# A vision transformer block on one core: patches and norm weights as half-precision parts, gates as value columns, stacked context parts, scores of four heads at once, a new order

## The chip, the cores and the metric

The program runs on one core of one Trainium2 chip. The time is the device time of that core for one launch, which computes 128 images; three runs of the kernel before are at hand. TensorE does the matrix products, VectorE, ScalarE and GpSimd (POOL in the rows) the rest, and SyncE issues the transfers.

## The reference

Each image of 224 x 224 x 3 is cut into 196 patches of 16 x 16, and the real part of each patch's Fourier transform, weighted, is projected to 192 numbers. With a class token that gives 197 tokens (T). Two layers follow, each added to what went in: attention with 12 heads of 16, whose softmax runs over the queries (`axis=2`), and attention with 12 heads of 64, with a norm on each head's queries and keys, and gates per head.

```python
x_fft = jnp.fft.rfft2(patches, norm='ortho').real            # times freq weights
out = jnp.concatenate([cls, x_flat @ proj_w.T + proj_b], axis=1) + pos_emb
# first layer, on _layernorm(h)
probs = jax.nn.softmax(scores, axis=2)                       # heads of 16
h = h + einsum('bhqk,bhke->bhqe', probs, v) @ Wo + bo
# second layer, on x = _layernorm(h)
q, k = _layernorm(q, w, b), _layernorm(k, w, b)              # per head of 64
attn = softmax((q * scale) @ k.T, axis=-1)
gates = softmax(x @ wg_w), top 2 of 10; softmax(x @ wg1_w); softmax(x @ wg0_w)
h = h + (gates * (attn @ v)) @ proj_w + proj_b
```

## The kernel before, in words

The tokens of an image lie in two chunks of 99 (TC); 198 (TP) columns hold both. Each of the five programs (`pe`, `dve`, `act`, `pool`, and SyncE's) runs a loop over the images, and the order of its steps is written out by hand in the table `ORDER`: `3:s1_0` is step `s1` number 0 of the image three ahead of the loop's own. So four images are in work at once, in different stages. Engines meet by semaphores alone: `made` waits until TensorE has filled a use of a PSUM bank, `read_out` and `room_for` until a reader has emptied it. The digits behind `@` in the table of `pe` are the banks (0 to 7) that a step fills. A step that waits holds up all that stands behind it on its engine.

The steps of an image, in the order of its data:

- `load` (SyncE) brings `xa` and `xb`, each pixel and its mirror, as 4 chunks of 98 rows (KC, KR). `fold` (VectorE, L877) adds them to `xs`, single precision. `tok` (TensorE) multiplies `xs` with `weff`, single precision, 4 chunks for each of the two token chunks. `tok` on VectorE (L883) adds positions and takes the moments for the layer norm (`moments`, L853 to L862): the statistics of two halves of a row, put together with six small instructions. `root1` (GpSimd, L440) is the inverse root. `nx1` (VectorE) normalises into two half-precision parts, high and low (`parts`).
- `x1T`, `qk1_0` to `qk1_2`, `v1`: transposes and products of the first layer. `mm5` forms a product of high and low parts in five half-precision passes (L491).
- `s1_0` to `s1_11`: scores of a head of the first layer, on 32 rows of the array, two heads at once, in four matmuls each. VectorE takes the maximum (L903), ScalarE the exponential with its sum (L733) into `p1`.
- `ctx_0` to `ctx_2`: VectorE scales `v1` by the inverse sums into `vs1` (L914, 16 of 32 columns per head, the rest zero), TensorE multiplies with `p1`, ScalarE copies the high part to `ctxT` and `cl` (L1015) the low part. `wo` (18 matmuls: high by high, low by high, high by low) and its moments (L924) follow, then `nx2`, `x2T`.
- `qk0` to `qk5`, `sq` (GpSimd, L479) and `ms` (mean squares of the heads), `var0` to `var2` (L759 to L764 on ScalarE, L984 to L988 on VectorE: an inverse root with one refinement step), then `rstd` (TensorE spreads the roots by `sel_rstd`) and `qkn` (L996, VectorE: times the weight `ln_w`, times `qkc`), `bias` (GpSimd, L484).
- `gl` (10 matmuls with 14 columns) gives the gate logits; `gl` and `gate` on VectorE make the gates from them.
- `v2` (values), `s2`, maximum (L1002) and exponential (L771) of the second layer, `gr` (gate over sum), `sc` (GpSimd, L475), `pT` (transposes, L672), `o2`, `ol`, and `proj`, which ends in the result and the store.

Outside the loop the weights are loaded and split once. The program is filled and drained by rounds of the same loop in which steps of images that don't exist are left out (`run_phases`).

## Time and profile before

| | us |
|---|---|
| median of three runs | 5535.41 (5534.62 to 5535.42) |
| span of the profiled execution | 5532.4 |
| TensorE busy in it | 5344.4 |
| VectorE busy | 4923.8 |
| ScalarE busy | 4327.1 |
| GpSimd busy | 2985.7 |
| one image in the loop (`tok` to `tok`) | 42.01 |

All times are of one execution on the one core. A busy time is the time in which at least one instruction of the engine is in work, so instructions that overlap count once; the mean length of an instruction is therefore longer than the distance from one to the next. In a timeline, instructions of one kind that follow each other stand in one row with their count, and the distance of two rows' starts is what the first of them took of the engine.

### The profile page before, as it was taken

How to read it: one execution, taken by the hardware profiler on the slowest of the kernel's cores; microseconds unless marked ns; L12 is line 12 of the kernel's file. 1: busy time of each engine (PE TensorE's matmuls, PEld its weight loads, DVE VectorE, ACT ScalarE, POOL GpSimd, SP SyncE). 2: the span in 40 equal slices, each digit the busy share in tenths (PEclk: the TensorE clock that was granted, in tenths of full speed). 3: DMA queues.
4: the chain of work that ended last, by engine and by line, in shares of the span. 5: the costliest groups of instructions: out<-in, count | busy, mean ns of one | idle time of the engine just before them, and what ended most of it. 6: DMA issues, size and time to landing. Idle time of an engine off the chain costs nothing.

```text
span 5532.4 us, 202492 instructions
## 1 busy us (share of the span) xinstructions
PE 5344.4 (97%) x63024; PEld 4563.7 (82%) x63024; DVE 4923.8 (89%) x16193; ACT 4327.1 (78%) x17409; POOL 2985.7 (54%) x3206
## 2 busy tenths in 40 slices
...
GB/s 72 18 22 18 17 21 17 18 17 21 18 17 21 17 18 17 21 18 17 21 18 17 20 18 18 17 21 18 17 21 17 18 17 21 18 17 21 18 17 6
...
## 3 DMA queue, kind: packets, MB, share of 16 engines
...
q14 instruction: 26, 0.21, 0.0%
...
## 4 chain that ended last, share of the span: by engine, by line
PE 94%; DVE 4%; issue 1%; ACT 0%; POOL 0%; SPq 0%; DVEq 0%; DMA 0%; POOLq 0%; ACTq 0%
PE bank L491 82%; PE bank L672 10%; PE bank L529 2%; DVE qk L898 1%; DVE qkn L996 1%; SPq L403 0%; ACT p L733 0%; DMA bp<-in_bp 0%; ACT pq L771 0%; POOL pq L475 0%; DVEq L902 0%; DVEq L1025 0%; DVE wqk_mean L804 0%; DVEq L992 0%; DVE nmax L903 0%
## 5 line engine op out<-in xcount | busy, mean ns | idle before, releaser
L475 POOL TENSOR_TENSOR pq<-pq,gn 99x788 f32<-99x788 f32 x768 | 1153.3, 1502 | 914.0 <-DVE gn L1011 913.9
L771 ACT ACTIVATE pq<-bank,nmax 99x197 f32<-99x197 f32 x3072 | 1300.1, 453 | 291.6 <-DVE nmax L1002 291.6
L733 ACT ACTIVATE p<-bank,nmax 99x197 f32<-99x197 f32 x3072 | 1323.1, 467 | 112.0 <-DVE nmax L903 97.3
L484 POOL TENSOR_TENSOR qkb<-qkn,ln_b 128x396 f32<-128x396 f32 x768 | 639.5, 847 | 1164.0 <-DVE qkn L996 1151.4
L777 ACT ACTIVATE pT<-bank 99x394 f32<-99x394 f32 x1536 | 767.6, 518 | 259.4 <-PE bank L672 256.4
L903 DVE TENSOR_REDUCE nmax<-bank 99x2 f32<-99x394 f32 x1536 | 843.2, 563 | 113.9 <-PE bank L491 101.7
L1002 DVE TENSOR_REDUCE nmax<-bank 99x2 f32<-99x394 f32 x1536 | 827.2, 559 | 25.7 <-PE bank L491 10.7
L733 ACT ACTIVATION_READ_ACCUMULATOR p<-bank,nmax 99x1 f32 x3072 | 762.6, 248 | 0.0
L491 PE MATMUL bank<-x2T,wqkc 128*128 128x198 f16 (+1 forms) x7680 | 752.5, 248 | 1.0 <-ACT p L733 0.7
L672 PE MATMUL bank<-ident,pq 99*99 99x99 f32 (+1 forms) x6144 | 725.3, 253 | 7.7 <-ACT pq L771 5.2
L771 ACT ACTIVATION_READ_ACCUMULATOR pq<-bank,nmax 99x1 f32 x3072 | 720.7, 235 | 0.0
L479 POOL TENSOR_TENSOR sq<-qkc 128x396 f32<-128x396 f32 x768 | 645.5, 848 | 103.0 <-ACT qkc L745 96.5
L491 PEld LDWEIGHTS bank<-x2T,wqkc 128*128 128x128 f16 (+1 forms) x7680 | 654.8, 97 | 51.5 <-issue 33.1
L672 PEld LDWEIGHTS bank<-ident,pq 99*99 99x99 f32 (+1 forms) x6144 | 626.7, 166 | 64.3 <-issue 38.3
L491 PE MATMUL bank<-qkb 64*99 64x197 f32 x6144 | 672.2, 345 | 6.8 <-POOL qkb L484 6.8
L996 DVE SCALAR_TENSOR_TENSOR qkn<-bank,ln_w,qkc 128x198 f32<-128x198 f32 x1536 | 568.2, 417 | 44.3 <-PE bank L491 38.0
L491 PE MATMUL bank<-pT,v 128*64 128x197 f32 x6144 | 600.8, 337 | 0.0
L491 PEld LDWEIGHTS bank<-qkb 64*99 64x99 f32 x6144 | 462.1, 162 | 135.9 <-issue 78.6
L491 PEld LDWEIGHTS bank<-pT,v 128*64 128x64 f32 x6144 | 407.7, 137 | 141.4 <-issue 72.9
L491 PE MATMUL bank<-wv,x2T 128*99 128x384 f16 (+1 forms) x2560 | 491.6, 331 | 0.0
L491 PE MATMUL bank<-qk 32*99 32x197 f16 x6144 | 374.4, 254 | 75.9 <-DVE qk L898 69.0
L782 ACT ACTIVATE oT<-bank 128x197 f16<-128x197 f32 x768 | 277.3, 361 | 169.1 <-PE bank L491 169.1
...
## 6 DMA issues: line engine op xcount, KB each, us to landing
xa<-in_xa SPq DMA_DIRECT2D x128, 300.1 KB
xb<-in_xb SPq DMA_DIRECT2D x128, 300.1 KB
out_tokens<-res SPq DMA_DIRECT2D x128, 74.2 KB
out_tokens<-res SPq DMA_DIRECT2D x128, 73.5 KB
...
```

The source lines that it names most:

```text
L475: nc.gpsimd.tensor_tensor(pair, pair, factor, op=ALU.mult).then_inc(s_sc.up(), 1)
L479: nc.gpsimd.tensor_tensor(sq[:, t], qkc[:, t], qkc[:, t], op=ALU.mult).then_inc(s_sq.up(), 1)
L484: nc.gpsimd.tensor_tensor(qkb[:, t], qkn[:, t % QKN_SLOTS], ln_b[:].unsqueeze(2).to_broadcast([128, 2, TP]), op=ALU.add).then_inc(s_qk.up( ...
L491: return nc.tensor.matmul(o, l, r, start=first, stop=last)
L672: last = nc.tensor.transpose(o[0:TC, k * T + c * TC:k * T + c * TC + n], pq[0:n, h % SLOTS, c, k * TC:k * TC + TC], ident[0:n, 0:n])
L733: last = nc.scalar.activation(p1[0:TC, h, c, :], psum("s1", h)[0:TC, c * T:c * T + T], ACT.Exp, bias=nmax1[:, c, h:h + 1], accum_out=sum1[ ...
L771: last = nc.scalar.activation(pq[0:TC, h % SLOTS, c, 0:T], psum("s2", h)[0:TC, c * T:c * T + T], ACT.Exp, bias=nmax2[:, h, c:c + 1], accum ...
L777: nc.scalar.activation(pT[0:TC, h].rearrange("p a b -> p (a b)"), psum("pT", h)[0:TC, 0:2 * T], ACT.Copy).then_inc(free("pT", h), 1)
L782: nc.scalar.activation(oT[:, t, 0, 0:T], psum("o2", t)[:, 0:T], ACT.Copy).then_inc(s_oh.up(), 1)
L903: V.tensor_reduce(nmax1[:, :, h], psum("s1", h)[0:TC, 0:2 * T].rearrange("p (a b) -> p a b", a=2), op=ALU.max, axis=AX.X, negate=True).the ...
L996: last = V.scalar_tensor_tensor(qkn[:, t % QKN_SLOTS, s, :], psum("rstd", t)[:, s * TP:s * TP + TP], ln_w[:, s:s + 1], qkc[:, t, s, :], AL ...
L1002: V.tensor_reduce(nmax2[:, h, :], psum("s2", h)[0:TC, 0:2 * T].rearrange("p (a b) -> p a b", a=2), op=ALU.max, axis=AX.X, negate=True).the ...
```

## The change

It has seven parts.

- **Patches.** The folded rows are laid out as 4 chunks of 128 rows instead of 98: three full ones, and the remaining rows twice in the fourth. `fold` moves to GpSimd and adds in place; a new step `xhi` (ScalarE) writes the half-precision high part `xh`, a new step `xlo` (GpSimd) the low part `xl`. `weff` is split the same way (`weff`, `weff_low`, scaled by 256). `tok` on TensorE becomes 22 half-precision matmuls instead of 8 single-precision ones (16 in the trace, which shows each as two).
- **Norm weights.** `ln_w` is multiplied into `sel_rstd` as two half-precision parts at the start, so that `qkn` is one product of 396 columns instead of two of 198 with a weight.
- **Gates.** The 14 columns of the gate weights stand behind the second layer's value weights: `gl` on TensorE goes, two of the four `v2` get 398 columns, and VectorE reads the logits from `v2`.
- **Context.** `vs1` holds each head's 16 columns twice, so that one product gives them on 32 rows; `cl` subtracts the high part from the lower half alone, `ctxT` then holds both parts in one operand, and `wo` has 12 matmuls.
- **First scores.** `s1` takes four heads at once, in four banks.
- **Moments.** The halves' statistics are put together by the aggregate instruction.
- **Order.** The table is new; `tok` runs four images ahead, and SyncE's loop is in the table too.

```diff
 def tok(img, _):
-    pe.wait_ge(*s_fold.at(img, 1))
+    pe.wait_ge(*s_xl.at(img, 1))
     for c in range(2):
-        for k in range(KC):
-            last = mm(o[0:TC, c * D:c * D + D], xs[:, k, c * TC:c * TC + TC], weff[:, k, :], k == 0, k == KC - 1)
+        tokens = slice(c * TC, c * TC + TC)
+        products = [(xh[:, 3, tokens], weff[:, 3, :]), (xl[:, 3, tokens], weff[:, 3, :])]
+        for k in range(KC - 1):
+            products += [(xh[:, k, tokens], weff[:, k, :]), (xh[:, k, tokens], weff_low[:, k, :]), (xl[:, k, tokens], weff[:, k, :])]
...
+def fold(img, _):
+    pool.wait_ge(*s_load.at(img, 32))
+    nc.gpsimd.tensor_tensor(xa[:], xa[:], xb[:], op=ALU.add).then_inc(s_fold.up(), 1)
+def xlo(img, _):
+    pool.wait_ge(*s_xh.at(img, 1))
+    nc.gpsimd.tensor_tensor(xl[:, :, 1:T], xa[:], xh[:, :, 1:T], op=ALU.subtract).then_inc(s_xl.up(), 1)
...
+def xhi(img, _):
+    act.wait_ge(*s_fold.at(img, 1))
+    if not isinstance(img, int) or img > 0:
+        act.wait_ge(*made(img - 1, "tok", 0))
+    nc.scalar.activation(xh[:, :, 1:T], xa[:], ACT.Copy).then_inc(s_xh.up(), 1)
...
 def s1(img, h):
-    if h % 2:
+    if h % GROUP:
         return
-    heads = (h, h + 1)
+    heads = range(h, h + GROUP)
...
 def wo(img, _):
-        for n, (x, w) in enumerate(((0, 0), (1, 0), (0, 1))):
+        for w in range(2):
             for g in range(3):
-                last = mm(o[0:TC, c * D:c * D + D], ctxT[:, g, x, c * TC:c * TC + TC], wo1[:, w, g, :], n + g == 0, n + g == 4)
+                last = mm(o[0:TC, c * D:c * D + D], ctxT[:, g, 1, c * TC:c * TC + TC], wo1[:, w, g, :], w + g == 0, w + g == 3)
...
 def v2_(img, n):
-    last = mm5(o[0:TC, 0:384], lambda k, r: wv2[r, k, 384 * a:384 * a + 384], lambda k, r: x2T[r, k, c, :], False)
+    cols = 384 + a * NG
+    last = mm5(o[0:TC, 0:cols], lambda k, r: wv2[r, k, 384 * a:384 * a + cols], lambda k, r: x2T[r, k, c, :], False)
...
 def moments(img, layer, src, name):
-    V.tensor_tensor(both[n][:], halves[:, :, 0, 1:3], halves[:, :, 1, 1:3], op=ALU.add)
...
+    V.memset(vare[n][:], LN_EPS)
+    for c in range(2):
+        last = V.bn_aggr(both[n][:, c, :], stats[n][:, c, :])
+    step(last, img, name, 2)
+    V.tensor_tensor(vare[n][:], both[n][:, :, 1], vare[n][:], op=ALU.add).then_inc(s_mv[layer].up(), 1)
...
 def rstd_(img, t):
-    for s in range(2):
-        last = V.scalar_tensor_tensor(qkn[:, t % QKN_SLOTS, s, :], psum("rstd", t)[:, s * TP:s * TP + TP], ln_w[:, s:s + 1],
-                                      qkc[:, t, s, :], ALU.mult, ALU.mult)
+    V.tensor_tensor(qkn[:, t % QKN_SLOTS].rearrange("p a b -> p (a b)"), psum("rstd", t)[:, 0:2 * TP],
+                    qkc[:, t].rearrange("p a b -> p (a b)"), op=ALU.mult).then_inc(free("rstd", t), 1)
...
 def load(img, _):
-    sp.wait_ge(*s_fold.at(img, 0))
+    sp.wait_ge(*s_xl.at(img, 0))
...
 ORDER, "pe":
-3:s1_6@15 1:s2_6@06 2:qk2@4 1:rstd5@7 1:pT_2@2 2:qk3@1 2:gl@0 3:s1_8@34 2:qk4@7 2:qk5@0 1:pT_3@6 3:s1_10@53 1:s2_8@12
+2:qk2@3 2:qk3@6 1:pT_6@4 3:s1_4@1572 1:pT_7@3 2:qk4@0 2:qk5@6 1:s2_10@31 1:o2_0@4 1:o2_1@5 1:o2_2@7 2:ms0@6 2:ms1
```

Three places of the order follow. A built program shows single-precision matmuls once, where the trace shows two; `s1` writes from `qk` (tile `qk1`), `s2` from `qkb`, the transposes `pT` from `ident,pq`, `qk` from `x2T,wqkc`.

TensorE before, the scores of two pairs of heads (`s1_8`, `s1_10`) in the middle of the loop:

```order
L491 MATMUL bank<-x2T,wqkc 128x198 x10
L491 MATMUL bank<-wgate,x2T 99x14 x10
L491 MATMUL bank<-qk 99x197 x8
L491 MATMUL bank<-x2T,wqkc 128x198 x20
L672 MATMUL bank<-ident,pq 99x99
L672 MATMUL bank<-ident,pq 99x98
L672 MATMUL bank<-ident,pq 99x99
L672 MATMUL bank<-ident,pq 99x98
L491 MATMUL bank<-qk 99x197 x8
L491 MATMUL bank<-qkb 99x197 x4
```

TensorE after, the scores of `s1_4` to `s1_7`:

```order
L521 MATMUL bank<-x2T,wqkc 128x198 x20
L698 MATMUL bank<-ident,pq 99x99
L698 MATMUL bank<-ident,pq 99x98
L698 MATMUL bank<-ident,pq 99x99
L698 MATMUL bank<-ident,pq 99x98
L521 MATMUL bank<-qk 99x197 x16
L698 MATMUL bank<-ident,pq 99x99
L698 MATMUL bank<-ident,pq 99x98
L698 MATMUL bank<-ident,pq 99x99
L698 MATMUL bank<-ident,pq 99x98
L521 MATMUL bank<-x2T,wqkc 128x198 x20
L521 MATMUL bank<-qkb 99x197 x4
```

Two groups of eight matmuls with other work between them became one group of sixteen; the gate product `wgate` is gone.

GpSimd before, the squares and the products with the gates (`sc`), then the roots of the layer norms and the first `bias` steps of the next round:

```order
L479 TENSOR_TENSOR sq<-qkc 128x396 x3
L475 TENSOR_TENSOR pq<-pq,gn 99x4x197
L479 TENSOR_TENSOR sq<-qkc 128x396
L475 TENSOR_TENSOR pq<-pq,gn 99x4x197 x2
L440 TENSOR_TENSOR rstd<-vare,mhalf 99x2
L484 TENSOR_TENSOR qkb<-qkn,ln_b 128x396 x2
L440 TENSOR_TENSOR rstd<-vare,mhalf 99x2
L484 TENSOR_TENSOR qkb<-qkn,ln_b 128x396
L452 TENSOR_TENSOR h1b<-h,bo 99x192 x2
```

GpSimd after, the end of a round of its list, from `sc4` to `sc1` of the next:

```order
L505 TENSOR_TENSOR pq<-pq,gn 99x4x197 x2
L514 TENSOR_TENSOR qkb<-qkn,ln_b 128x396
L458 TENSOR_TENSOR xa<-xa,xb 128x784
L514 TENSOR_TENSOR qkb<-qkn,ln_b 128x396
L490 TENSOR_TENSOR h2b<-h,bp 99x192 x2
L514 TENSOR_TENSOR qkb<-qkn,ln_b 128x396
L463 TENSOR_TENSOR xl<-xa,xh 128x4x196
L514 TENSOR_TENSOR qkb<-qkn,ln_b 128x396 x2
L505 TENSOR_TENSOR pq<-pq,gn 99x4x197 x2
```

The fold and the low part stand between the `bias` steps (`qkb`), and all of these come behind one another.

VectorE before, around the refinement of the head variance (`lnvar` to `rs_hl`, step `var2`), with the low parts of the contexts ahead and `rsum`, `gn` (step `gr5`) behind:

```order
L1015 TENSOR_TENSOR ctxT<-bank,ctxT 128x197 x3
L1019 TENSOR_TENSOR oT<-bank,oT 128x197
L1002 TENSOR_REDUCE nmax<-bank 99x2
L877 TENSOR_TENSOR xs<-xa,xb 98x4x196
L984 SCALAR_TENSOR_TENSOR lnvar<-bank,rootsq 128x198
L986 SCALAR_TENSOR_TENSOR rootsq<-lnvar,root 128x198
L987 TENSOR_SCALAR rs_mask<-rootsq,low_rows 128x198
L988 SCALAR_TENSOR_TENSOR rs_hl<-rootsq,rs_mask 128x198
L1008 RECIPROCAL rsum<-sum 99x4
L1011 TENSOR_TENSOR gn<-rsum,mg 99x4
L1019 TENSOR_TENSOR oT<-bank,oT 128x197
L924 SCALAR_TENSOR_TENSOR h<-bank,h1b 99x384
```

VectorE after, the same step:

```order
L1056 TENSOR_TENSOR oT<-bank,oT 128x197
L1044 RECIPROCAL rsum<-sum 99x4
L1047 TENSOR_TENSOR gn<-rsum,mg 99x4
L1056 TENSOR_TENSOR oT<-bank,oT 128x197 x2
L1022 SCALAR_TENSOR_TENSOR lnvar<-bank,rootsq 128x198
L1024 SCALAR_TENSOR_TENSOR rootsq<-lnvar,root 128x198
L1025 TENSOR_SCALAR rs_mask<-rootsq,low_rows 128x198
L1026 SCALAR_TENSOR_TENSOR rs_hl<-rootsq,rs_mask 128x198
L1056 TENSOR_TENSOR oT<-bank,oT 128x197
L1015 TENSOR_SCALAR v<-bank 99x384
L1033 TENSOR_TENSOR qkn<-bank,qkc 128x396
L929 COPY x1T<-bank 128x396
```

The fold ahead of it is gone; behind it stand now the low part of an output, a `v2` and the first `qkn` of the same image, for which TensorE needs the result of this step.

## Rows read from the trace of the kernel before

**Rows 1.** The page, part 1: busy time, share of the span and instructions of each engine.

```profile
PE 5344.4 (97%) x63024; PEld 4563.7 (82%) x63024; DVE 4923.8 (89%) x16193; ACT 4327.1 (78%) x17409; POOL 2985.7 (54%) x3206
```

**Rows 2.** One steady image: stretch, length, busy by engine, clock, DMA share, GB/s.

```profile
2422.77:2464.78 42.01, 41.45 (x495) 35.47 (x493) 38.08 (x127) 33.77 (x138) 23.26 (x25) 1.00 0.06 18
```

**Rows 3.** Timeline of TensorE: start, length (us), line, operation, tiles, [idle before].

```profile
2410.23 0.60 PE L491 MATMUL bank<-wgate,x2T 128*99 128x14 f16 x10
2410.76 0.54 PE L491 MATMUL bank<-qk 32*99 32x197 f16 x8
2411.23 1.91 PE L491 MATMUL bank<-x2T,wqkc 128*128 128x198 f16 x20
...
2418.90 0.85 PE L491 MATMUL bank<-p,vs 128*32 128x197 f32 x16
2419.68 0.89 PE L491 MATMUL bank<-pT,v 128*64 128x197 f32 x8
2420.51 0.94 PE L672 MATMUL bank<-ident,pq 99*99 99x99 f32 x8
2421.28 1.65 PE L491 MATMUL bank<-wo,ctxT 128*99 128x192 f16 x18
2422.77 2.77 PE L491 MATMUL bank<-weff,xs 98*99 98x192 f32 x16
2425.38 0.51 PE L672 MATMUL bank<-ident,pq 99*99 99x99 f32 x4
2425.72 0.33 PE L491 MATMUL bank<-rs_hl,sel_rstd 128*128 128x198 f16 x2
...
2432.24 1.02 PE L491 MATMUL bank<-wv,x2T 128*99 128x384 f16 x5
2433.10 0.52 PE L529 MATMUL bank<-ident,parts 99*128 99x99 f16 x8
2433.45 3.14 PE L491 MATMUL bank<-wp,oT 128*99 128x192 f16 x36
...
2439.05 0.76 PE L491 MATMUL bank<-qk 32*99 32x197 f16 x16 [0.56 <-DVE qk L898]
2439.74 0.91 PE L491 MATMUL bank<-qkb 64*99 64x197 f32 x8
```

**Rows 4.** Timeline of VectorE, same columns, from the fold to a layer norm.

```profile
2421.22 0.97 DVE L877 TENSOR_TENSOR xs<-xa,xb 98x784 f32<-98x784 f32 x1
2422.10 0.36 DVE L984 SCALAR_TENSOR_TENSOR lnvar<-bank,rootsq 128x198 f32<-128x198 f32 x1
...
2423.71 0.18 DVE L1008 RECIPROCAL rsum<-sum 99x4 f32<-99x4 f32 x1
...
2425.55 0.16 DVE L857 TENSOR_TENSOR both<-stats 99x4 f32<-99x4 f32 x1
...
2426.36 1.45 DVE L996 SCALAR_TENSOR_TENSOR qkn<-bank,ln_w,qkc 128x198 f32<-128x198 f32 x4
2427.73 0.55 DVE L883 TENSOR_TENSOR h<-bank,posb 99x384 f32<-99x384 f32 x1
```

**Rows 5.** Timeline of VectorE, one pair of the `vs` products.

```profile
2412.26 0.83 DVE L914 TENSOR_TENSOR vs<-v,rsum 99x64 f32<-99x64 f32 x2
```

**Rows 6.** Timeline of GpSimd at the same time.

```profile
2412.02 0.85 POOL L479 TENSOR_TENSOR sq<-qkc 128x396 f32<-128x396 f32 x1
```

**Rows 7.** Groups by line and shape, VectorE: busy us, mean ns of one, idle before.

```profile
L914 DVE TENSOR_TENSOR vs<-v,rsum 99x64 f32<-99x64 f32 x384 | 154.5, 402 | 23.8
...
L914 DVE TENSOR_TENSOR vs<-v,rsum 98x64 f32<-98x64 f32 x384 | 82.0, 214 | 0.0
```

**Rows 8.** The page, part 5: GpSimd's longest product, same columns.

```profile
L475 POOL TENSOR_TENSOR pq<-pq,gn 99x788 f32<-99x788 f32 x768 | 1153.3, 1502 | 914.0 <-DVE gn L1011 913.9
```

**Rows 9.** Timeline of ScalarE, the head variance and what follows.

```profile
2420.05 0.42 ACT L759 ACTIVATE lnvar<-bank,eps 128x198 f32<-128x198 f32 x1
...
2421.18 0.48 ACT L777 ACTIVATE pT<-bank 99x394 f32<-99x394 f32 x1
```

More of the change, by code:

```diff
@@ L60, in fold_pairs, with fold_rows @@
     return np.array(first), np.array(mirror)
+def fold_rows(rows):
+    out = np.zeros((KC * KR, *rows.shape[1:]), np.float32)
+    out[:3 * KR] = rows[:3 * KR]
+    rest = rows[3 * KR:]
+    for part in range(2):
+        out[3 * KR + 64 * part:3 * KR + 64 * part + len(rest)] = rest
+    return out
 def fold_basis():
@@ L137 @@
+3:v1@4 1:pT_1@2 1:pT_2@3 1:s2_6@56 1:pT_3@0 2:x2T@2 3:qk1_2@3 1:s2_8@10 2:qk0@2 2:qk1@5 1:pT_4@4 1:rstd5@6 1:pT_5@2
+2:qk2@3 2:qk3@6 1:pT_6@4 3:s1_4@1572 1:pT_7@3 2:qk4@0 2:qk5@6 1:s2_10@31 1:o2_0@4 1:o2_1@5 1:o2_2@7 2:ms0@6 2:ms1
+2:ms2 3:ctx0@0 1:o2_3@4 4:x1T@3 2:v2_0@1 1:pT_8@5 2:rstd0@7 1:pT_9@2 1:pT_10@6 1:pT_11@4 2:rstd1@5 3:s1_8@2137
+1:o2_4@0 1:o2_5@6 2:s2_0@54 2:v2_1@0 2:v2_2@2 2:rstd2@6 2:v2_3@1 2:rstd3@0
 """,
     "dve": """
-3:fold 1:var2 0:gr5 0:ol1 2:wo 1:rstd0 1:rstd1 3:tok 0:ol2 0:ol3 0:ol4 3:nx1 0:ol5 1:s2_0 1:s2_1 1:gate3 1:s2_2 1:s2_3
@@ L149 @@
 """,
     "pool": """
-3:root1 1:bias2 3:h1b 1:h2c 2:h2b 1:sc0 1:sc1 1:bias3 2:sq0 1:sc2 2:sq1 1:bias4 1:bias5 2:sq2 2:sq3 2:sq4 1:sc3 2:sq5
-1:sc4 1:sc5 3:root2 2:bias0 2:bias1
+0:sc0 0:sc1 1:root2 0:h2c 2:h1b 0:sc2 0:sc3 1:sq0 1:sq1 1:sq2 0:bias5 3:root1 1:sq3 1:sq4 1:sq5 0:sc4 0:sc5 1:bias0
+4:fold 1:bias1 1:h2b 1:bias2 4:xlo 1:bias3 1:bias4
+""",
+    "sp": """
+4:load 0:store
 """,
```

184 lines of the change are left out of this document (92 added, 92 removed).

## The prediction

> **What bounds the kernel now.** I read the busy shares first, then one steady image, then the waits inside it. The page puts TensorE at 97% of the span, VectorE at 89%, ScalarE at 78%, GpSimd at 54% [rows 1]. The ends matter little with 128 images, so the number to explain is the length of one image in the loop, from one `tok` to the next: 42.01 us [rows 2]. In it TensorE is busy 41.45 us, VectorE 38.08, ScalarE 33.77, GpSimd 23.26, and the granted clock is 1.00, the 2.4 GHz level [rows 2]. What TensorE does not do in that time is 0.56 us, and the timeline shows it as one wait, ahead of the sixteen `s1` matmuls, for VectorE's `qk1` [rows 3]. So work taken off TensorE shortens the image, until VectorE (91% full) or a hand-over between engines takes its place. The span is 5532.4 us against a median of 5535.4, so 3 us are added at the end; 128 images of 42.01 are 5377.3, which leaves 155.1 us for loading, preparing, filling and draining.
>
> **TensorE, part by part.** Costs are taken from the start of one group to the start of the next, because a matmul's own length overlaps its neighbours.
> `tok`: 2422.77 to 2425.38, 2.61 us in single precision [rows 3]. After, it is 22 half-precision products with 192 moving columns. The 18 of `wo` have that shape and run from 2421.28 to 2422.77, 1.49 us or 0.083 each [rows 3]. 22 x 0.083 = 1.82: minus 0.79.
> `wo`: 18 become 12: minus 0.50.
> `gl`: 2410.23 to 2410.76, 0.53 us, disappears [rows 3]. Ten `v2` matmuls get 14 more columns, at 0.083/192 us a column 0.06: minus 0.47.
> `s1`: a pair of heads alone takes 2410.76 to 2411.23, 0.47 us, and stands alone four times in the image; the two pairs that follow each other take 2439.05 to 2439.74, 0.69 us [rows 3]. That is 4 x 0.47 + 0.69 = 2.57. After, there are three groups of four heads. What a group costs no row shows exactly. It can't be under the 0.47 of a pair, since each head still has four matmuls behind each other; the nearest upper row is the 0.69 of two pairs one after the other. So the term lies between 1.41 and 2.07. I take 0.47, because in the 0.69 row the second pair's instructions stand behind all of the first pair's, while the new loop alternates the four heads, as the pair alternates its two: minus 1.16, at worst minus 0.50.
> `ctx` keeps its 32 columns per head, so its matmuls cost what they did; folding the norm weights into `sel_rstd` changes no matmul. I count 21 changes of tile shape (full, row parts, column parts) in the order of before and 20 after, and take them as equal.
> Sum: 41.45 - 0.79 - 0.50 - 0.47 - 1.16 = 38.5 us of TensorE work an image; 39.2 with the dear `s1`.
>
> **The other engines.** VectorE loses the fold, 2421.22 to 2422.10: minus 0.88 [rows 4]. Its twelve `qkn` products (four in 2426.36 to 2427.73, 0.34 each) become six of 396 columns; the 384-column `h` shows 0.55 as a length, so six take at most 3.3 instead of 4.1, and less where they follow closely [rows 4]: minus 0.8 to 1.2, I take 1.0. The two layer norms run from `both` to the next work in 2425.55 to 2426.36, 0.81 us, with six small instructions [rows 4]; after it is four. The aggregate of the statistics stands in no row: as cheap as the small ones the saving is 0.54 for both layers, with a longer one it is nothing; I take 0.5. The scaled `vs` doubles its 64 columns in six instructions; from 0.21 for 64 [rows 7] to 0.55 for 384 a column costs 1.06 ns, so plus 0.4. VectorE: 38.08 - 0.88 - 1.0 - 0.5 + 0.4 = 36.1 us, 92% of a 39.2 us image: nearly as full as now. Gates read from SBUF and the other edits of `tok` and `cl` keep their shapes: zero.
> ScalarE gets `xhi`, 784 columns, some 1.0 us as twice the 0.48 of a 394-column copy [rows 9]: 34.8. GpSimd gets the fold and `xlo`, each near the 1502 ns of its 788-column product [rows 8]: 26.3 of 39.2, 67%. Behind `fold` and `xlo` on GpSimd stand `bias1` to `bias4`, for which `s2` waits; at 12 us of slack an image I put no cost on them. SP's loads now wait for `xlo` and stand in one queue with the stores; `fold` comes at the end of the next round of GpSimd's list, most of an image after the store that the load stands behind, so nothing. They carry 128 rows for 98.
>
> **What is late next.** The order is new, so every cushion is. The narrowest that I find is the head variance. TensorE's `ms2` ends, ScalarE does `var0` and `var1` (2420.05 to 2421.18, and 0.1 to finish: 1.2 us [rows 9]), VectorE does `var2` (2422.10 to 2423.71, 1.5 to 1.6 [rows 4]), and TensorE's `rstd0` waits for that: 2.8 us, and three hand-overs. Before, `ms2` ends at 2418.90 and `rstd0` starts at 2425.72, 6.8 us later [rows 3]. After, five steps stand between them: `ctx` 0.78, `o2` 0.83, `x1T` 0.35, `v2` 0.86, `pT` 0.34 [rows 3], 3.16 in all. That leaves 0.0 to 0.4, if VectorE is free at once. Besides, four banks must be free at each `s1` group where two were enough. The waits of TensorE lie between nothing and some 2 us an image (every `s1` group and `rstd0` late by 0.5). I take 0.7, near the 0.56 that the row of before shows, because the engine that makes TensorE wait is as full as it was.
>
> **The time.** 38.5 + 0.7 = 39.2 us an image, 128 of them 5018. Filling and draining: 155 now; one more phase, and fold, `xhi` and `xlo` ahead of the first `tok` (4 us) against shorter phases: 130 to 170, I take 150. With the 3 us of the median: 5018 + 150 + 3 = 5171, say **5170 us**, 6.6% less.
>
> **Rivals.**
> *No wait is left.* TensorE goes through in 38.5: 128 x 38.5 + 153 = 5081. For it: one wait in an image now. Against: the 3.16 us cushion.
> *Four heads don't run at once.* Then `s1` costs 0.69 or more a group, the image 39.9, the time 5260. For it: the only row with two pairs together. Against: the alternation.
> *VectorE stands behind GpSimd and becomes the bound.* At 2412.26 VectorE's pair of `vs` products, with two SBUF inputs, takes 0.83 us, and GpSimd is in `sq` from 2412.02 for 0.85, so until 2412.87 [rows 5, 6]. Over the run the first of such a pair takes 402 ns, the second 214 [rows 7]: 0.19 more, three times an image. After, GpSimd is busy for 67% instead of 55%, with longer instructions, and such products (three `vs`, two `parts`, two in `var2`) meet it in other places. If seven are held by 0.6 us, less the 0.56 paid now, VectorE needs 36.1 + 3.6 = 39.7, and with 0.6 of its own waits the image is 40.3, the time 5311. The Trainium skill, SBUF — State Buffer, section "Who interferes with whom", says that a VectorE instruction with two SBUF inputs and a GpSimd instruction that reads SBUF shut each other out, the second waiting for the whole of the first; this trace agrees (0.83 us ending with `sq`). By that rule the new placing alone decides, which the rows can't tell.
> *Slower: the four banks.* If TensorE stands at each `s1` group until the fourth bank has been read, and nothing behind it may pass, then 42.05 - 38.5 = 3.5 us of waiting, 1.2 at each of three groups, makes the time equal to now (5535), and 1.5 at each gives an image of 43.0 and 5657. For it: the single wait of the trace is at such a group [rows 3]. Against: it is 0.56, and the banks are taken by work that ends a microsecond and more ahead. The Trainium skill, TensorEngine Tiling (Array Packing), "Gotcha 1: PSUM Pressure", warns of this: different row tiles write different banks. Here a row shows 0.56 for two pairs and none shows four taken at once.
>
> **Chances.** Forecast (image 38.9 to 39.6, 5130 to 5220) 0.47; no wait 0.25; `s1` dear 0.08; VectorE behind GpSimd 0.13; the four banks 0.04; about the same time, by several small delays, 0.03. Differences under 0.2% can't be told from none. Faster 0.93, same 0.03, slower 0.04. The range runs from 5060 (38.4 us, filling 145) to 5315, which takes in all rivals but the slower ones and the outer halves of two.
>
> **What would show it.** In the profile after: the image from `tok` to `tok` at 39.2; `tok` near 1.8 us, `wo` 1.0, a group of sixteen `s1` matmuls near 0.5 (0.69: the dear case); VectorE near 36 us busy an image; TensorE's waits at `rstd` behind VectorE's `rs_hl` or at `s1`, 0.7 us together. VectorE at 97% or more, `vs` with a mean above 0.6, would be the lock; waits above 1 us at each `s1` group the banks. I am wrong if the image stays above 40 with TensorE idle, or if the granted clock falls below the upper level in the loop.

## The result: slower, 6117.6 us, and the profile after

The changed kernel takes 6117.57 us (median of 4 runs, 6116.84 to 6117.92) beside 5535.1 for the kernel before on the same chip: 1.1052 times as long, interval 1.1037 to 1.1068. Forecast was 5170, and 5060 to 5315 as range. An image takes 46.64 us instead of 42.01.

The page of after, part 1, answers [rows 1]; then one steady image from one `tok` to the next, in the columns of [rows 2]:

```profile
PE 5135.4 (84%) x61744; PEld 4202.8 (69%) x61744; DVE 5640.8 (92%) x14799; ACT 4465.3 (73%) x17537; POOL 3433.0 (56%) x3462
```

```profile
3019.06:3065.70 46.64, 39.79 (x485) 32.57 (x484) 43.80 (x116) 34.86 (x138) 26.75 (x28) 1.00 0.06 20
```

TensorE's work did shrink (41.45 to 39.79 us busy), ScalarE and GpSimd have what was forecast (34.86, 26.75), and the clock stays at 1.00, the 2.4 GHz level. VectorE, forecast at 36.1 us, is busy for 43.80. TensorE is idle for 6.85 us an image, no longer in one wait as in [rows 3] but in waits of six kinds. Its waits over the whole run (us in total, times, longest):

```profile
PE bank L521 <- ACT p L766: 273.7, 248, 2.3
PE bank L521 <- DVE oT L1056: 199.2, 250, 1.4
PE bank L521 <- DVE qkn L1033: 118.7, 126, 2.4
PE bank L521 <- DVE ctxT L1051: 118.3, 126, 1.8
PE bank L563 <- DVE parts L913: 105.4, 129, 6.0
PE bank L521 <- DVE rs_hl L1026: 54.3, 128, 0.9
```

Five of them name VectorE. The first names ScalarE's `p`, which itself stood 951.1 us behind VectorE's `nmax` (page, part 5):

```profile
L766 ACT ACTIVATE p<-bank,nmax 99x197 f32<-99x197 f32 x3072 | 1276.9, 433 | 951.2 <-DVE nmax L939 951.1
```

So the waits lead to VectorE. VectorE itself is idle for 2.84 us of the image, 1.67 of it in one wait for ScalarE's `pq`. It has not more instructions than before (14799 for 16193) but longer ones. Its groups by line and shape, the columns of [rows 7]:

```profile
L1047 DVE TENSOR_TENSOR gn<-rsum,mg 99x4 f32<-99x4 f32 x768 | 499.9, 651 | 26.3
L909 DVE TENSOR_SCALAR x<-h,both,rstd 99x192 f32<-99x192 f32 x512 | 396.6, 814 | 1.5 <-POOL rstd L468 1.5
L951 DVE TENSOR_TENSOR vs<-v,rsum 98x128 f32<-98x128 f32 x384 | 315.7, 822 | 0.0
L912 DVE CAST parts<-x 99x384 f16<-99x384 f32 x256 | 275.5, 1076 | 8.8
L1024 DVE SCALAR_TENSOR_TENSOR rootsq<-lnvar,root 128x198 f32<-128x198 f32 x128 | 120.5, 941 | 4.4
L983 DVE TENSOR_TENSOR glog<-v,gmax 99x20 f32<-99x20 f32 x128 | 103.8, 811 | 0.0
```

In the trace of before, `gn` of the same shape took 166 ns, `x` 374, the conversion 386, `rootsq` 367. Instructions that read PSUM did not grow (`nmax` 559 ns, as before; `qkn`, whose shape is new, 560). Nor did GpSimd's own products (`pq` 1504 ns for 1502, `sq` 851 for 848): the standing still is VectorE's. One `gn`, a product of four columns, on VectorE's timeline, and GpSimd's at the same time (start, length, as [rows 3]):

```profile
3040.14 0.18 DVE L1044 RECIPROCAL rsum<-sum 99x4 f32<-99x4 f32 x1 [1.67 <-ACT pq L804]
3040.36 1.81 DVE L1047 TENSOR_TENSOR gn<-rsum,mg 99x4 f32<-99x4 f32 x1
3042.09 1.98 DVE L939 TENSOR_REDUCE nmax<-bank 99x2 f32<-99x394 f32 x4
```

```profile
3038.89 2.46 POOL L509 TENSOR_TENSOR sq<-qkc 128x396 f32<-128x396 f32 x3
3041.30 0.85 POOL L514 TENSOR_TENSOR qkb<-qkn,ln_b 128x396 f32<-128x396 f32 x1
3042.11 0.70 POOL L468 TENSOR_TENSOR rstd<-vare,mhalf 99x2 f32<-99x2 f32 x1
```

`gn` begins at 3040.36, inside the second square, and ends at 3042.17, with the end of `qkb` (3042.15). This is what [rows 5] and [rows 6] showed for `vs` and one `sq`, now over the rest of a square, a whole one and a bias.

### The profile page after: what moved, and what is told of

Its sections match the earlier page's. It is cut to its first block, busy times and chain, and to the rows that moved or that the text cites. A ratio compares the mean times of both kernels' runs of the same rounds, so it can differ in the third digit from the quotient of the medians.

```text
span 6116.0 us, 195587 instructions
## 1 busy us (share of the span) xinstructions
PE 5135.4 (84%) x61744; PEld 4202.8 (69%) x61744; DVE 5640.8 (92%) x14799; ACT 4465.3 (73%) x17537; POOL 3433.0 (56%) x3462
## 4 chain that ended last, share of the span: by engine, by line
DVE 57%; issue 25%; PE 10%; ACT 5%; DVEq 2%; ACTq 0%; POOL 0%; POOLq 0%
DVE nmax L939 11%; PE bank L521 8%; DVE x L909 6%; DVE nmax L1038 5%; DVE parts L912 5%; DVE oT L1056 4%; DVE qkn L1033 4%; ACT pq L804 4%; DVE v L1015 3%; DVE ctxT L1051 2%; DVE vs L951 2%; DVE rootsq L1024 2%; DVE parts L913 1%; DVE rsum L1044 1%; PE bank L563 1%
## 5 line engine op out<-in xcount | busy, mean ns | idle before, releaser
L766 ACT ACTIVATE p<-bank,nmax 99x197 f32<-99x197 f32 x3072 | 1276.9, 433 | 951.2 <-DVE nmax L939 951.1
L505 POOL TENSOR_TENSOR pq<-pq,gn 99x788 f32<-99x788 f32 x768 | 1154.9, 1504 | 947.0 <-DVE gn L1047 934.6
L1038 DVE TENSOR_REDUCE nmax<-bank 99x2 f32<-99x394 f32 x1536 | 837.6, 559 | 8.6 <-PE bank L521 8.4
L939 DVE TENSOR_REDUCE nmax<-bank 99x2 f32<-99x394 f32 x1536 | 802.7, 556 | 8.5 <-PE bank L521 8.5
L810 ACT ACTIVATE pT<-bank 99x394 f32<-99x394 f32 x1536 | 725.2, 515 | 116.1 <-PE bank L698 106.2
L698 PE MATMUL bank<-ident,pq 99*99 99x99 f32 (+1 forms) x6144 | 750.6, 254 | 4.4 <-POOL pq L505 3.8
L521 PE MATMUL bank<-x2T,wqkc 128*128 128x198 f16 (+1 forms) x7680 | 731.9, 248 | 0.4 <-DVE x2T L971 0.2
L766 ACT ACTIVATION_READ_ACCUMULATOR p<-bank,nmax 99x1 f32 x3072 | 651.7, 212 | 0.0
L1047 DVE TENSOR_TENSOR gn<-rsum,mg 99x4 f32<-99x4 f32 x768 | 499.9, 651 | 26.3
L521 PE MATMUL bank<-wv,x2T 128*99 128x384 f16 (+3 forms) x2560 | 494.0, 331 | 29.2 <-DVE oT L1056 29.2
L815 ACT ACTIVATE oT<-bank 128x197 f16<-128x197 f32 x768 | 263.2, 372 | 282.5 <-PE bank L521 282.5
L1033 DVE TENSOR_TENSOR qkn<-bank,qkc 128x396 f32<-128x396 f32 x768 | 429.9, 560 | 13.2 <-PE bank L521 3.2
```

What stands on the lines that cost most here:

```text
L505: nc.gpsimd.tensor_tensor(pair, pair, factor, op=ALU.mult).then_inc(s_sc.up(), 1)
L521: return nc.tensor.matmul(o, l, r, start=first, stop=last)
L698: last = nc.tensor.transpose(o[0:TC, k * T + c * TC:k * T + c * TC + n], pq[0:n, h % SLOTS, c, k * TC:k * TC + TC], ident[0:n, 0:n])
L766: last = nc.scalar.activation(p1[0:TC, h, c, :], psum("s1", h)[0:TC, c * T:c * T + T], ACT.Exp, bias=nmax1[:, c, h:h + 1], accum_out=sum1[ ...
L810: nc.scalar.activation(pT[0:TC, h].rearrange("p a b -> p (a b)"), psum("pT", h)[0:TC, 0:2 * T], ACT.Copy).then_inc(free("pT", h), 1)
L939: V.tensor_reduce(nmax1[:, :, h], psum("s1", h)[0:TC, 0:2 * T].rearrange("p (a b) -> p a b", a=2), op=ALU.max, axis=AX.X, negate=True).the ...
```

## The experiments

**Theories.** L (for lock): VectorE's instructions from SBUF to SBUF stand still while GpSimd's run. O: the new order, its hand-overs and the four banks cost the time. Q: GpSimd's list is longer, so its results come too late, whatever VectorE does. Every kernel was timed beside the kernel before (5535 to 5537 us in each set). Image lengths are medians from `tok` to `tok`; where a busy time or a time is given by the image, it is that of the whole run by 128. `...` marks what is cut from an edit; signals at the ends of lines are left out in some.

### GpSimd taken out of the way

**Slivers.** Every product of GpSimd's loop on two columns (a sliver), for instance:

```
- nc.gpsimd.tensor_tensor(sq[:, t], qkc[:, t], qkc[:, t], op=ALU.mult)
+ nc.gpsimd.tensor_tensor(sq[:, t, 0, 0:2], qkc[:, t, 0, 0:2], qkc[:, t, 0, 0:2], op=ALU.mult)
```

> The changed kernel, in which each of GpSimd's products in the loop (folding, low part, scaling, squares, biases) works on two columns only; the rest of each product is left out, every wait and signal stays. Theory L (VectorE's products from SBUF to SBUF stand still while GpSimd's products run, some 10 us of its 46.6 us an image): VectorE has some 35 us of work left, TensorE's 38.5 us bound it again, 39 to 40 us an image, 5080 to 5270 us in all; gn falls from 651 to below 250 ns, the scaled values from 822 to below 450. Theory O (the new order and the hand-overs between engines, with the matrix results in fewer free banks, cost the time): GpSimd's length hardly matters, above 5800 us.

Measured: 5141.85 us, 38.93 us an image. Its steady image and its groups:

```profile
3012.84:3051.77 38.93, 38.93 (x484) 32.73 (x483) 34.74 (x117) 34.44 (x138) 5.87 (x27) 1.00 0.07 25
```

```profile
L909 DVE TENSOR_SCALAR x<-h,both,rstd 99x192 f32<-99x192 f32 x512 | 169.1, 373 | 1.5 <-POOL rstd L468 1.5
L1047 DVE TENSOR_TENSOR gn<-rsum,mg 99x4 f32<-99x4 f32 x768 | 125.1, 163 | 26.4
L951 DVE TENSOR_TENSOR vs<-v,rsum 98x128 f32<-98x128 f32 x384 | 109.3, 285 | 0.0
L912 DVE CAST parts<-x 99x384 f16<-99x384 f32 x256 | 98.5, 385 | 8.8
```

TensorE is busy without a gap in the same order with the same banks: O falls as a cause by itself. Busy time after less busy time here, by 128 images, prices the standing still: `gn` 2.93 us an image, `x` 1.78, `vs` 1.66, the conversion 1.38, `glog` 0.95, `rootsq` 0.58: 9.3 us. (VectorE's busy time of the whole image is 9.06 us longer; neighbours overlap.) L and Q are both still open, since GpSimd is short here.

**Fills.** GpSimd at least as busy as in the changed kernel (4153.5 us for 3433.0), but almost only writing (`filler` is a spare tile that brings the length up, the sliver carries the wait):

```
- nc.gpsimd.tensor_tensor(sq[:, t], qkc[:, t], qkc[:, t], op=ALU.mult).then_inc(s_sq.up(), 1)
+ nc.gpsimd.tensor_tensor(tiny[0:128, 6 + t], qkc[:, t, 0, 0:2], qkc[:, t, 0, 0:2], op=ALU.mult)
+ nc.gpsimd.memset(filler[:, 5410 + 600 * t:6010 + 600 * t], 1.0)
+ nc.gpsimd.memset(sq[:, t], 1.0).then_inc(s_sq.up(), 1)
```

> The changed kernel, in which GpSimd's products in the loop are replaced by fills of about the same length, which only write SBUF (a product of two columns stands ahead of each for the wait): the arithmetic of these steps is left out, and GpSimd is busy as long as before. Theory L, in which the two engines are in each other's way when both read: VectorE's gn below 300 ns, the second product of the scaled values below 450 ns, and 5080 to 5400 us. Theory Q (GpSimd's queue is simply longer, and its results come later): as slow as the changed kernel, above 5900 us, gn still near 651 ns.

Measured: 5911.94 us (mean granted clock 0.968), the time of Q with the `gn` of L. The groups fall into two kinds:

```profile
L924 DVE TENSOR_SCALAR x<-h,both,rstd 99x192 f32<-99x192 f32 x512 | 712.6, 1431 | 10.1 <-POOL rstd L474 2.3
L927 DVE CAST parts<-x 99x384 f16<-99x384 f32 x256 | 189.3, 740 | 8.8
L1062 DVE TENSOR_TENSOR gn<-rsum,mg 99x4 f32<-99x4 f32 x768 | 125.2, 163 | 26.2
L966 DVE TENSOR_TENSOR vs<-v,rsum 98x128 f32<-98x128 f32 x384 | 109.1, 284 | 0.0
```

Products with two SBUF operands are free (163, 284 ns, as with slivers). Those with one SBUF operand and a scalar or none are held: `x` longer than in the changed kernel (1431 ns for 814), the conversion less long (740 for 1076), and `rs_mask`, a third of that form, which was free there, takes 677 ns for 326. The Trainium skill, SBUF — State Buffer, section "Who interferes with whom", says both: a VectorE instruction with two SBUF inputs contends with a GpSimd instruction that reads SBUF, not with one that only writes; copies, conversions and tensor-scalar forms can enter a mode that uses both ports, and in it they contend with GpSimd. These rows agree, and in the changed kernel instructions of both kinds are held.

**Fills, and no form that fills hold.** The fills trimmed to the products' lengths, and `x`, its conversion and `rs_mask` given a second operand:

```
- last = V.tensor_scalar(dst[:, c, :], src[:, c, :], both[layer][:, c, 0:1], rstd[layer][:, c:c + 1],
-                        ALU.subtract, ALU.mult)
+ last = V.scalar_tensor_tensor(dst[:, c, :], src[:, c, :], both[layer][:, c, 0:1],
+                        rstd[layer][:, c:c + 1].to_broadcast([TC, D]), ALU.subtract, ALU.mult)
...
```

> The changed kernel, in which GpSimd's products in the loop are again fills that only write SBUF (the arithmetic of these steps is left out), with lengths nearer to the products' own, and in which VectorE's x, its conversion to half precision and rs_mask have a second operand instead of a scalar or none. In the run with fills alone just these three forms were still held (x 1431 ns) and the two-operand products were not. Theory L (VectorE standing still is the cost): nothing is held, x below 420 ns, 5130 to 5350 us. Theory Q (GpSimd's results come too late, whatever VectorE does): 5700 us or more. In between, the excess over 5142 us is GpSimd's lateness and the rest of the 975 us is the standing still.

Measured: 5201.80 us, 39.38 us an image:

```profile
3005.84:3045.22 39.38, 39.24 (x484) 32.60 (x483) 35.36 (x117) 34.63 (x138) 27.39 (x72) 1.00 0.07 24
```

```profile
L924 DVE SCALAR_TENSOR_TENSOR x<-h,both,rstd 99x192 f32<-99x192 f32 x512 | 189.1, 411 | 1.6 <-POOL rstd L474 1.6
```

GpSimd is as busy (27.39 us) as in the changed kernel (26.75), in the same places, and TensorE is full again. So Q costs 60 us at most (5202 less 5142, with VectorE's work 0.62 us an image longer by the three changed forms), and L the other 916 of the 976 us between the changed kernel and the slivers. This decides between the three.

**Only the new work short.** Slivers for the folding and the low part alone:

```
- nc.gpsimd.tensor_tensor(xa[:], xa[:], xb[:], op=ALU.add)
+ nc.gpsimd.tensor_tensor(xa[:, 0, 0:2], xa[:, 0, 0:2], xb[:, 0, 0:2], op=ALU.add)
...
```

> The changed kernel, in which only GpSimd's two new products, the folding and the low part, work on two columns (the rest of these two is left out); scaling, squares and biases are whole and stand where the change put them. This splits the 975 us between the changed kernel and the one with slivers for all. If the new work is what costs: 5142 to 5500 us. If the new places of the old work are: only the scaled values (1.66 us an image) and the gate logits (0.9 us) are freed, 43.5 to 45.5 us an image, 5720 to 5980 us.

Measured: 5795.38 us, 44.14 us an image:

```profile
3032.58:3076.72 44.14, 39.58 (x485) 32.66 (x484) 41.26 (x117) 34.60 (x138) 23.66 (x27) 1.00 0.06 22
```

`vs` and `glog` are free (2.6 us an image by their busy time), `gn`, `x`, the conversion and `rootsq` are held as in the changed kernel (651, 809, 1078, 941 ns), and the image is 2.50 us shorter: this standing still comes back one for one. Of the 976 us, 322 come from GpSimd's new work and 654 from work that it had before, now in other places.

### The whole arithmetic, out of GpSimd's way

**Standing back.** Two waits on GpSimd and two gates moved on VectorE:

```
  def square(img, t):
+     if t == 3 and (not isinstance(img, int) or img + 2 < images):
+         pool.wait_ge(*s_x1.at(img + 2, 1))
  def fold(img, _):
      pool.wait_ge(*s_load.at(img, 32))
+     if not isinstance(img, int) or img > 1:
+         pool.wait_ge(*s_vs.at(img - 2, 2))
- 3:s1_0 1:gr0 1:gr1 3:s1_1 3:s1_2 2:wo 0:proj
+ 3:s1_0 1:gr0 3:s1_1 3:s1_2 2:wo 1:gr1 0:proj
- 1:s2_9 1:gr4 3:s1_4 3:s1_5 3:s1_6 3:s1_7 3:ctx0 1:s2_10 1:s2_11 4:nx1
+ 1:s2_9 3:s1_4 3:s1_5 3:s1_6 3:s1_7 3:ctx0 1:s2_10 1:s2_11 1:gr4 4:nx1
```

> The changed kernel with the same arithmetic, only moved: GpSimd's fourth square waits until the patches' normalised values two images on are ready, its folding waits until the second scaled values are made, and on VectorE gr1 goes behind wo, gr4 behind s2_11. Theory L: about half of the 10 us that VectorE stands still goes, 41 to 44 us an image, 5400 to 5780 us. Theory O: no gain, or the added waits make it slower, above 6000 us.

Measured: 6051.14 us, where O had put it, but for a reason that the trace shows. VectorE's busy time fell to 4841.6 us, by 6.2 us an image, and the time by 0.5. VectorE now waited:

```profile
DVE lnvar L1026 <- ACT rootsq L801: 388.4, 127, 4.8
DVE nmax L943 <- PE bank L525: 225.2, 130, 3.8
DVE x L913 <- POOL rstd L470: 156.7, 128, 1.8
```

That is 6.0 us an image: the delayed square delays the mean squares of TensorE, those the roots of ScalarE (its `lnvar` waits 347.1 us for TensorE), and those VectorE's `lnvar`. **Without the square's wait** (that line alone taken out again):

> The kernel with GpSimd standing back, without its wait ahead of the fourth square (VectorE then waited 3 us an image for the roots): left are gr1 behind wo, gr4 behind s2_11, and the folding after the second scaled values. Theory L: gn is no longer held, x still is; 43 to 45 us an image, 5650 to 5900 us. If the order is what costs, moving two gates does not help: above 6050 us.

Measured: 5922.75 us, above L's range and below O's. VectorE's busy time fell by 4.3 us an image and the time by 1.5; the mean clock was 0.969, and TensorE's busy time for the same matmuls rose by 106 us (5241.7 against 5135.4).

**Squares on ScalarE**, read from the bank behind the copy, in the changed kernel's order:

```
...
+ nc.scalar.activation(sq[:, t].rearrange("p a b -> p (a b)"), psum("qk", t)[:, 0:2 * TP], ACT.Square,
+                      scale=1.0 / W_SCALE).then_inc(free("qk", t), 1)
- nc.gpsimd.tensor_tensor(sq[:, t], qkc[:, t], qkc[:, t], op=ALU.mult)
...
```

> The changed kernel with its order and the same results; only the six squares an image go from GpSimd (0.85 us each, 5.1 us an image) to ScalarE, as a second reading of the bank behind its copy (some 0.4 us each, 2.5 us an image on an engine that was busy 73%). Theory L: the standing still that squares caused (some 4 of the 10 us of the image looked at: x, gn, rootsq) goes, 42 to 44.5 us an image, 5500 to 5850 us. Theory O (order and banks): no gain, or slower by ScalarE's longer queue, above 6050 us.

Measured: 5964.30 us, a gain of 153, above L's range and below O's. VectorE's busy time fell by 4.0 us an image, and its wait for ScalarE's `pq` ahead of `rsum` grew from 217.9 to 403.0 us in all.

**`gn` on GpSimd**, the folding behind `bias1`, the gate logits behind `s2_5` (and ScalarE's exponential of them, `gate0`, behind its `s2_4`):

```
- V.tensor_tensor(gn[:, heads, :], rsum2[:, heads, :], mg[:, heads, :], op=ALU.mult)
+ nc.gpsimd.tensor_tensor(gn[:, heads, :], rsum2[:, heads, :], mg[:, heads, :], op=ALU.mult)
- 4:fold 1:bias1 1:h2b 1:bias2
+ 1:bias1 4:fold 1:h2b 1:bias2
- 1:s2_3 1:gl 1:s2_4 2:cl1 1:s2_5
+ 1:s2_3 1:s2_4 2:cl1 1:s2_5 1:gl
- 0:gate0 0:s2_3 0:s2_4
+ 0:s2_3 0:s2_4 0:gate0
```

> The same without the step to ScalarE: gn on GpSimd, the folding behind bias1, the gate logits behind s2_5; x and its conversion (3.2 us of standing still an image) stay on VectorE. Theory L: 41.5 to 44 us an image, 5460 to 5780 us, between the changed kernel and the one with x on ScalarE. Theory O: above 5950 us.

Measured: 5579.48 us, 42.35 us an image, as L had it: 538 us less than the changed kernel, with all its arithmetic, and still 1.0077 times the kernel before (1.0057 to 1.0097). What is left is visible, a sum of two columns for example, on VectorE's and then GpSimd's timeline:

```profile
3018.61 1.26 DVE L907 TENSOR_TENSOR vare<-both,vare 99x2 f32<-99x2 f32 x1
```

```profile
3018.35 1.50 POOL L509 TENSOR_TENSOR pq<-pq,gn 99x788 f32<-99x788 f32 x1
```

**That, and `x` on ScalarE** (two scaled copies and the conversion, with a shift that VectorE and GpSimd prepare; VectorE keeps the low part):

```
+ nc.scalar.activation(dst[:, c, :], src[:, c, :], ACT.Identity, bias=shift[layer][:, c:c + 1], scale=rstd[layer][:, c:c + 1])
+ nc.scalar.activation(parts[layer][:, :, 0:D, 0], dst[:], ACT.Copy)
...
```

> The changed kernel with the same results and its whole arithmetic, in which the products that stood still are taken out of GpSimd's way: gn goes to GpSimd itself (six products of some 0.2 us an image); the folding comes behind bias1, where VectorE reads PSUM; the shifted gate logits come behind s2_5; and x with its high part goes to ScalarE (two scaled copies and a conversion for each layer, some 2.6 us an image), so that VectorE keeps the low part only. By the busy times gn, the scaled values, x, its conversion and the logits lose together 8.7 us of standing still an image. Theory L: TensorE bounds again, 39.4 to 41 us an image, 5190 to 5420 us, below the kernel before. Theory O (the order and its banks, which stay as they are): above 5800 us.

Measured: 5828.39 us, a miss for L; the number lies where O had put it, the trace shows why. VectorE is busy for 4340.2 us only, and waits for ScalarE instead (4.3 us an image):

```profile
DVE parts L933 <- ACT parts L756: 548.8, 256, 2.9
```

**Three more places freed**, from the run with `gn` on GpSimd (the small constant added on GpSimd, `gr5` behind `var2`, `gr4` behind `nx1`); then, apart, **`s2_6` ahead of `nx2` as well** (the last pair of lines) and **the squares on ScalarE as well** (the edit above):

```
+ nc.gpsimd.tensor_tensor(vare[layer][:], both[layer][:, :, 1], epsp[:], op=ALU.add)
- 1:ol0 1:gr5 1:ol1 1:ol2 2:var2 1:ol3
+ 1:ol0 1:ol1 1:ol2 2:var2 1:gr5 1:ol3
- 1:s2_9 1:gr4 3:s1_4 3:s1_5 3:s1_6 3:s1_7 3:ctx0 1:s2_10 1:s2_11 4:nx1
+ 1:s2_9 3:s1_4 3:s1_5 3:s1_6 3:s1_7 3:ctx0 1:s2_10 1:s2_11 4:nx1 1:gr4
- 2:nx2 1:gr2 1:s2_6 3:qk1_1
+ 1:s2_6 2:nx2 1:gr2 3:qk1_1
```

> The kernel with gn on GpSimd, with three more places taken out of GpSimd's way, results and arithmetic kept: the small constant is added to the variance on GpSimd (VectorE's sum was held 1.10 us an image by a scaling), gr5 goes behind var2 (rootsq was held 0.89 us) and gr4 behind nx1 (the low part was held 1.15 us). Theory L: 3.1 of the remaining 5.2 us of standing still go; 39.6 to 41.0 us an image, 5220 to 5400 us. Theory O: the time stays near 5580 us, above 5500 us, since the order's places and the banks stay.

> The same, and s2_6 (a product from PSUM) ahead of nx2, so that VectorE reads PSUM while GpSimd writes h2c and h1b, which hold x and its conversion by some 1.0 us an image. Theory L: up to 0.5 us an image less than without, 5150 to 5380 us; if the later x2 costs TensorE more than VectorE gains: up to 60 us slower than without.

> The first of these three with the squares on ScalarE, so that the second layer's x (held 1.06 us an image by two squares) is free. Theory L alone: 0.5 to 1 us an image faster than without, below 5330 us. ScalarE then has some 37 us of work an image: if it becomes what is waited for, slower than without by 50 us or more, as x on ScalarE was.

Measured: 5712.09, 5882.72 and 5997.63 us: L missed its range three times, and each run is slower than without its edits (for the last, one of the two expectations had said so). VectorE's busy time fell each time (4828.9, 4718.2, 4632.6 us against 4987.3 with `gn` on GpSimd), and TensorE waits elsewhere: for the scalings `pq` of GpSimd 155 to 156 us in each (4.6 with `gn` on GpSimd), and for `parts` 246.8 us in the second (143.7). In the first of the three TensorE waits 1.17 us for a scaling ahead of `pT`, and its clock goes with it. Stretches of one microsecond, in the columns of [rows 2]:

```profile
3019.00:3020.00 1.00, 0.83 (x10) 0.61 (x8) 1.00 (x4) 0.73 (x2) 0.47 (x2) 1.00 0.00 0
3020.00:3021.00 1.00, 0.21 (x3) 0.05 (x1) 1.00 (x4) 0.50 (x1) 1.00 (x1) 1.00 0.00 0
3021.00:3022.00 1.00, 0.62 (x5) 0.65 (x6) 0.96 (x3) 0.00 (x0) 1.00 (x2) 0.84 0.00 0
3022.00:3023.00 1.00, 1.00 (x11) 0.67 (x9) 0.39 (x2) 0.74 (x2) 0.04 (x1) 0.50 0.00 0
...
3025.00:3026.00 1.00, 1.00 (x14) 0.61 (x10) 0.26 (x1) 0.63 (x3) 1.00 (x1) 0.95 0.00 0
```

The granted clock is 0.50, the 1.2 GHz level, until 3025. Over this run it is 0.980 on the mean, and TensorE's busy time for the same matmuls is 98 us above that of the run with `gn` on GpSimd (5181.8 against 5083.8, clock 0.996); the three edits lost 133 us. The clock is not the whole of it: two of the three edits, next, lost 73 us at 0.995.

**One edit, then two.** The constant on GpSimd alone; then `gr5` behind `var2` as well:

> The kernel with gn on GpSimd, with one edit that moves nothing: the small constant is added to the variance on GpSimd (0.2 us) instead of on VectorE, whose sum was held 1.10 us an image by a scaling, on the way from h to x. Theory L: this sum's hold goes and no hand-over comes later, 41.2 to 42.0 us an image, 5420 to 5530 us, just below the kernel before. If the run with three edits lost by this one and not by its two moves: 5600 us or more.

> The same and gr5 behind var2, which ends the hold of rootsq (0.89 us an image) but lets the last scaling start some 1.5 us later. If standing still decides: 0.3 to 0.9 us an image less than without, 5310 to 5490 us. If the moves are what cost in the run with three edits: slower than without by 30 us or more.

Measured: 5599.67 and 5652.81 us, against 5579.48 without: both above L's ranges; that the second would lose by its move was the other expectation. In the first the sum's standing still is gone and another instruction has taken it over, GpSimd's list having shifted: the first `vs` of a pair goes from 307 to 640 ns.

```profile
L960 DVE TENSOR_TENSOR vs<-v,rsum 99x128 f32<-99x128 f32 x384 | 245.9, 640 | 24.6
```

In the second `rootsq` is free, and TensorE waits for the later scaling instead, 1.0 us an image:

```profile
PE bank L707 <- POOL pq L514: 130.3, 132, 2.1
```

### The parts in the old order

**Parts on the kernel before**: order and gates kept; context parts, norm weights, moments and half-precision patches taken over, the folding and the low part on VectorE, the first four `s1` together; then **all `s1` in pairs**; then **the squares on ScalarE**; then, from the second, **slivers** on GpSimd. The lists of VectorE (first three pairs) and ScalarE against before, and the step from the first kernel to the second:

```
- 3:fold 1:var2 0:gr5
+ 1:var2 0:gr5
- 3:s1_4 3:qk1_2 1:rstd3
+ 3:s1_4 3:qk1_2 4:fold 1:rstd3
- 1:s2_9 2:gate2 3:ctx2
+ 1:s2_9 2:gate2 4:xlo 3:ctx2
- 2:gate0 3:s1_8 2:qk3
+ 2:gate0 4:xhi 3:s1_8 2:qk3
```

```
- heads = range(h, h + (2 if h else 4))
+ heads = range(h, h + 2)
```

> The kernel before, its order and its gates kept, with these parts of the change: context parts stacked, norm weights in the spreading matrix, the moments by the aggregating instruction, patches as half-precision parts with the folding and the low part on VectorE (GpSimd gets no new work), and only the first four of the first scores together. TensorE by the prediction's terms: 41.45 less 0.79, 0.50 and a third of 1.16 is 39.8 us an image; VectorE 38.1 less 1.5 plus 0.9 is 37.5. Theory L: 40.3 us an image, 5280 to 5400 us. Theory O, or parts that are dearer on TensorE than forecast: 5450 us or more.

> The kernel in the old order with the parts, now with all first scores in pairs as before. In the run with the first four together the old order gave 42.4 us an image; TensorE waited there 1.3 us an image ahead of that group for ScalarE's p and pq (four banks wanted at once), and 0.55 us for scaled values held by a square. If that is so: 41.2 to 41.6 us an image, 5430 to 5490 us, faster than before by 1 to 2%. If the parts themselves cost in the old order: 5540 us or more.

> The kernel in the old order with the parts and with pairs, in which the squares go to ScalarE. In the run with pairs TensorE lost 1.7 us an image in waits (for p and pq of ScalarE, for scaled values that a square held, for qk), as much as the parts had saved. Theory L: the scaled values and gsel are no longer held (1.2 us an image by their spread), 41.0 to 41.8 us an image, 5400 to 5500 us. If ScalarE's queue is what the old order waits for, its 2.5 us more make it slower: 5600 us or more.

> The kernel in the old order with the parts and pairs, in which GpSimd's products in the loop work on two columns only (the rest is left out). In the old order VectorE does the folding and the low part, and by the trace it stands still 1.2 us an image (scaled values, gsel). Theory L: without it TensorE runs at its own 40.9 us an image (42.0 less 0.79, 0.50 and waits kept), 5330 to 5420 us. If the old order with the parts waits for ScalarE or VectorE whatever GpSimd does: above 5530 us.

Measured: 5594.26 (1.0105, 1.0088 to 1.0122), 5589.64, 5750.54 and 5418.23 us. The first two missed L's ranges: with GpSimd's products whole, the parts do not pay in the old order either. With pairs, the doubled `vs` take 477 and 492 ns (292 and 284 with slivers), and `gsel`, behind a scaling and a square, 842 for the 403 of before:

```profile
L958 DVE TENSOR_TENSOR vs<-v,rsum 98x128 f32<-98x128 f32 x384 | 188.8, 492 | 0.0
L1007 DVE TENSOR_TENSOR gsel<-gx,grest 99x20 f32<-99x20 f32 x128 | 107.8, 842 | 4.4
```

With slivers the image is 40.99 us, where L had put 40.9, and the time 0.9786 of the kernel before (0.9758 to 0.9815). So 171 us of the old order with the parts belong to GpSimd's products; how much of that is standing still and how much their lateness was not tried there. The squares on ScalarE made it slower (ScalarE's `p` is then the largest wait of TensorE, 128.8 us, and the clock is 0.973).

No version with the whole arithmetic beats the kernel before. The nearest is the one with `gn` on GpSimd, 0.8% slower.

## Why the prediction was wrong, point by point

- **The step that failed: VectorE's 36.1 us.** The sum took VectorE's instructions at the lengths that the rows of before show and added nothing more for standing still, though GpSimd got 3.5 us more work and all of its work moved. Measured are 43.80 us, 9.06 above the run with slivers. With it fell TensorE's waits of 0.7, taken "because the engine that makes TensorE wait is as full as it was": they are 6.85. What the prediction did ask of GpSimd's longer list, its lateness, was nearly right at "no cost": 60 us in all at most. Slack covers lateness, not what GpSimd does to VectorE while it works.
- **The rival with the right mechanism was sized at 4.2 us an image (seven holds of 0.6) and measured 9.3.** Its size failed by its list, not by its price. The seven that it counted cost 2.3 us together: `vs` 1.66, `rootsq` 0.58, the low parts 0.04, `rs_hl` nothing. It left out `gn` (2.93: six an image, 0.49 more each on the mean), the logits (0.95) and, because it looked for two SBUF operands only, `x` and its conversion (3.2). With 9.3 in place of 4.2 the rival's own sum would have been 36.1 + 9.3 - 0.56 + 0.6 = 45.4 us an image, near the 46.6 measured. Its reading of [rows 5, 6], "0.83 us ending with `sq`", is loose: 0.83 is both products of the pair; the first, 0.69 us long, ends 0.08 behind the square, the pair 0.22 behind it. Nor would its signs have named it: VectorE is busy for 94% of the image (97 asked for), and all `vs` together have a mean of 0.56 us (0.6), since the hold fell on the second of a pair.
- **TensorE's work: near.** In the slivers run, where nothing waits, an image is 38.93 us, forecast 38.5 of work. `tok` to the next step is 1.91 us (forecast 1.82), a group of sixteen `s1` matmuls 0.48 (0.47), `wo` 0.99 (1.0).
- **VectorE's own work: 36.1 forecast, 34.7 measured** in the same run. The aggregate takes 162 ns, as cheap as the small instructions; six `qkn` take 3.4 us.
- **GpSimd at 26.3: right** (26.75).
- **Chances.** The rival of VectorE behind GpSimd had 0.13 and a price that still ended below 5535, so all of slower was left to the banks at 0.04. That the rows can't tell what the new placing does was true, and should have widened the range: 654 of the 976 us are old work. In the old order the parts paid 171 us for GpSimd's products, so the new places cost some 480, an estimate from these two.
- **The four banks: not by themselves.** With slivers the groups of `s1` wait 4.7 us in the whole run; in the changed kernel 0.92 us an image, behind `ctxT` of the delayed VectorE.
- **The narrow cushion at `rstd0`, 0.0 to 0.4 us of spare time: it held where nothing stands still** (1.7 us of waiting behind `rs_hl` in the whole slivers run); in the changed kernel TensorE waits there 0.42 us an image.
- **Clock and filling: as forecast.** The clock stays at the upper level in the steady image; 6116.0 less 128 x 46.64 leaves 146 us, forecast 150.

The run with no hold took 5202 us, 32 from the forecast: the sum was near for a kernel without standing still, which the changed kernel is not.
